# Attention's shift moved out of a matrix product and into spare rows of its operands: a two-block transformer kernel on one Trainium2 core

## What is computed

```python
hd = emb // HEADS                       # 8, HEADS = 16
q = jnp.einsum('bse,oe->bso', x, wq) + bq
qh = q.reshape(HEADS, b, s, hd)
kh = qh
vh = qh
scores = jnp.einsum('hbqd,hbkd->hbqk', qh, kh) / sqrt(emb)
attn = jax.nn.softmax(scores, axis=-1)
out = jnp.einsum('hbqk,hbkd->hbqd', attn, vh)
...
x = x + 0.5 * ffn(ln(x))       # experts, "m0" in the kernel
x = x + attention(ln(x))       # this attention
x = x + 0.5 * ffn(ln(x))       # experts again, "m1"
```

## Time and profile before

| | us |
|---|---|
| median of three runs | 2499.76 |
| the profiled execution, its own time | 2515.66 |
| its span, first to last instruction | 2513.9 |
| outside the span | 1.8 |
| mean granted TensorE clock | 0.909 of full speed |
| TensorE busy | 2036.8 (81%) |
| VectorE busy | 1426.1 (57%) |
| ScalarE busy | 1236.0 (49%) |

### The profile page before, as it was taken

How to read it: one execution, slowest core, us unless ns; L and a number is a source line. 1 busy time by engine, 2 the same in 40 slices (tenths; PEclk the granted TensorE clock), 3 DMA queues, 4 the chain that set the end, 5 groups by cost and what they waited for, 6 DMA issues and landing times.

```text
span 2513.9 us, 38918 instructions
## 1 busy us (share of the span) xinstructions
PE 2036.8 (81%) x13610; PEld 1594.7 (63%) x13610; DVE 1426.1 (57%) x4130; ACT 1236.0 (49%) x2670; POOL 648.7 (26%) x663
## 2 busy tenths in 40 slices
PE   2766773587878888998899889989998999788884
PEld 1555552476557556875787578757875886665764
DVE  5877536453556675566556565666566356356522
ACT  3766413444446455555555564555455446335431
POOL 3111003333131133124223322332233124013052
PEclk9777885699889899999899999999999999899997
DMA  7100000112211211312132213221322312312121
GB/s 237 43 1 1 1 1 0 31 45 64 56 47 44 65 52 57 85 55 55 52 91 57 65 39 89 62 65 32 92 67 60 88 52 68 89 29 61 41 62 47
DMA packets 228948, 141.29 MB, mean 56 GB/s; under 512 B 116489, under 2 KB 206732, under 8 KB 228754
## 3 DMA queue, kind: packets, MB, share of 16 engines
q1 hardware_dynamic: 174320, 85.60, 13.4%
q0 software_dynamic: 16960, 34.74, 4.6%
q10 hardware_dynamic: 37474, 18.46, 2.6%
HBM read 82.48 MB, written 57.16 MB: 56 GB/s over the span
## 4 chain that ended last, share of the span: by engine, by line
PE 53%; DVE 24%; ACT 12%; issue 6%; DMA 2%; POOL 2%; SPq 1%; ACTq 0%; POOLq 0%; DVEq 0%
PE PS L908 17%; PE PS L876 9%; DVE AR L1085 3%; PE PS L1207 3%; PE PS L1170 3%; PE PS L1188 3%; PE PS L1433 2%; PE PS L1193 2%; ACT AR L1141 2%; DVE small L332 2%; ACT AR L837 2%; ACT AR L362 2%; DVE AR L795 2%; DVE xnT L1269 1%; PE PS L911 1%
## 5 line engine op out<-in xcount | busy, mean ns | idle before, releaser
L908 PE MATMUL PS<-AR,W 128*128 128x256 f32 x2560 | 653.0, 404 | 20.9 <-DVE AR L795 15.0
L795 DVE TENSOR_TENSOR AR<-AR,PS 128x512 f32<-128x512 f32 (+1 forms) x384 | 228.6, 597 | 653.9 <-ACT AR L837 525.8
L908 PEld LDWEIGHTS PS<-AR,W 128*128 128x128 f32 x2560 | 499.8, 204 | 92.1 <-issue 17.0
L837 ACT ACTIVATE AR<-PS 128x512 f32<-128x512 f32 (+1 forms) x384 | 201.1, 525 | 556.5 <-PE PS L908 439.1
L1085 DVE TENSOR_REDUCE AR<-PS 128x2 f32<-128x512 f32 x512 | 337.2, 688 | 160.0 <-PE PS L1170 155.6
L1141 ACT ACTIVATE AR<-PS 128x512 f32<-128x512 f32 x512 | 303.6, 600 | 236.3 <-PE PS L1193 231.9
L876 PE MATMUL PS<-AR,WO 128*128 128x256 f32 (+1 forms) x1536 | 357.7, 383 | 0.0
L876 PEld LDWEIGHTS PS<-AR,WO 128*128 128x128 f32 (+1 forms) x1536 | 295.5, 193 | 42.8
L1170 PE MATMUL PS<-AR 128*128 128x256 bf16 x1024 | 204.8, 287 | 40.4 <-DVE AR L1085 25.9
L743 POOL DMA_INDIRECT AR<-YE,gidx1c x128 | 128.8, 1007 | 379.8 <-issue 231.4
L743 POOL DMA_INDIRECT AR<-YE,gidx x128 | 128.3, 1002 | 350.9 <-ACT AR L1141 310.8
(11 more groups left out here) (359 smaller groups left out, 2771.5 us busy)
## 6 DMA issues: line engine op xcount, KB each, us to landing
AR<-XE SPq DMA_DIRECT2D x128, 128.0 KB, 2.1
YE<-AR ACTq DMA_DIRECT2D x128, 128.0 KB
AR<-QD SPq DMA_DIRECT2D x384, 32.0 KB
QD<-AR SPq DMA_DIRECT2D x8, 768.0 KB, 5.2
AR<-KD SPq DMA_DIRECT2D x64, 96.0 KB
W<-in_L_ffn_w_kernel_dram SPq DMA_DIRECT2D x2, 2560.0 KB, 13.5
OD<-AR SPq DMA_DIRECT2D x128, 36.0 KB
X<-in_L_attn_dense_dram SPq DMA_DIRECT2D x8, 512.0 KB, 4.5
```

What stands on the lines that cost most here:

```text
L795: ins = dve.tensor_tensor(hf[:, cols], gl[i % 2][:, cols], H[:, 2 * (i % 2) + 1, cols], ALU.mult)
L837: ins = act.activation(gl[i % 2][:, cols], H[:, 2 * (i % 2), cols], ACT.Gelu_apprx_tanh)
L908: mm = pe.matmul(H[:, b0, b * CAP:(b + 1) * CAP], w0[:, e, hb * P:(hb + 1) * P], xeT[e % 2], start=True, stop=True)
```

## The change

The shift goes into the operands. Rows 64 to 87 of the queries' image, unused so far, take the negated maxima: three parts for each of the 8 blocks. The keys' image holds a mask there that is 1 in the three rows of a key's own block and 0 in the others (`own`, written once for each of the 4 images by ScalarE, `own_act`). `shifted(i)` is then two matmuls, and the two with `pick` go. In detail:

- `scores` needs these rows to be zero in the queries, so each load of a piece has one more DMA, which copies 24 zero rows of the keys' image to them. The six DMAs of the queries become three, with a repeated source.
- `split` writes its parts in another layout; the transpose is two instead of one, and ScalarE's copy (`turned`) is 32x256 instead of 128x128.
- New on VectorE: `place(c)`, a copy of 32 partitions x 2048 bf16 that repeats the 256 negated maxima of each row for all 8 blocks. The first slot of a piece waits for it.
- The scores run up to 16 blocks ahead, and not 14.
- `split` of pieces 1 to 7 stands in slots 3, 8, 16, 24, 32, 40, 48 (before: 3, 11, 19, 27, 35, 43, 51), the transposes and `turned` two slots later, `values` in slots 7, 13, 21, 29, 37, 45, 53 (before: 2, 10, 18, ... 50), and `place` in slots 0, 8, 13, 21, 29, 37, 45, 53 for pieces 0 to 7.

```diff
         def scored(i):
-            return min(NS, i + PB + 6, PB + 2 * (i + 1))
+            return min(NS, i + 2 * PB, PB + 2 * (i + 1))
...
+        SPLIT = [slot_of(PB * (c + 2) - 1) for c in range(NPC - 1)]
+        TURN = [i + 2 for i in SPLIT]
+        VALUES = [TURN[0] + 2] + [i + 3 for i in TURN[1:]]
+        PLACE = [i + 5 for i in SPLIT]
...
-            for lo, hi, a in ((0, 8, 0), (8, 16, 0), (16, 24, 0), (24, 32, 8), (32, 40, 8), (40, 48, 16)):
-                sp.dma_start(QA[c % DEPTH][lo:hi, :], qr[a:a + hi - lo, :]).then_inc(S["a_kq%d" % (c % DEPTH)], 16)
+            for lo, times, part in ((0, 3, 0), (3 * AD, 2, 1), (5 * AD, 1, 2)):
+                rows = qr[part * AD:(part + 1) * AD].rearrange("(o d) t -> o d t", o=1)
+                sp.dma_start(QA[c % DEPTH][lo:lo + times * AD, :], rows.broadcast_to([times, AD, 2 * QUAD])
+                             ).then_inc(S["a_kq%d" % (c % DEPTH)], 16)
+            sp.dma_start(QA[c % DEPTH][SHIFT:SHIFT + 3 * PB, :],
+                         KA[c % DEPTH][ZEROS:ZEROS + 3 * PB].rearrange("p a t -> p (a t)")
+                         ).then_inc(S["a_kq%d" % (c % DEPTH)], 16)
...
+            def place(c):
+                dve.wait_ge(S["a_mp"], NPC * n + c + 1)
+                dve.tensor_copy(QA[c % DEPTH][SHIFTS, :].rearrange("p (g b t) -> p g b t", g=AH, b=PB),
+                                MP[c % 2][SHIFTS, :].rearrange("p (g o t) -> p g o t", g=AH, o=1).broadcast_to(
+                                    [32, AH, PB, AB])).then_inc(S["a_md"], 1)
...
+        def own_act(act, k):
+            view = KA[k][SHIFTS].rearrange("p g (x j) -> p g x j", j=4)
+            act.copy(view, own[SHIFTS, :].rearrange("p (g o j) -> p g o j", g=2, o=1).broadcast_to(
+                [32, 2, QUAD // 4, 4])).then_inc(S["a_kone"], 1)
...
-                act.wait_ge(S["a_mxT"], NPC * n + c + 1)
-                act.copy(MP[c % 2], turned_maxima(c)).then_inc(S["a_mp"], 1)
+                k = NPC * n + c
+                act.wait_ge(S["a_mxT"], k + 1)
+                if k >= 2:
+                    act.wait_ge(S["a_md"], k - 1)
+                act.copy(MP[c % 2][SHIFTS], turned_maxima(c)[SHIFTS]).then_inc(S["a_mp"], 1)
...
-                pe.transpose(turned_maxima(c), MS[c % 2].rearrange("p a b -> p (a b)"),
-                             identb[:, :]).then_inc(S["a_mxT"], 1)
+                for q in range(2):
+                    mm = pe.transpose(turned_maxima(c)[:, q * P:(q + 1) * P], MS[c % 2][:, q, :], identb[:, :])
+                mm.then_inc(S["a_mxT"], 1)
...
+                if b == 0:
+                    pe.wait_ge(S["a_md"], NPC * n + c + 1)
                 for h in range(2):
-                    pe.matmul(o[:, h * 256:(h + 1) * 256], keys(c, P, h, b), queries(c, b), start=(h == 0),
-                              stop=False, skip_group_check=True)
-                if b == 0:
-                    pe.wait_ge(S["a_mp"], NPC * n + c + 1)
-                for q in range(2):
-                    mm = pe.matmul(o.rearrange("p (h q t) -> p q h t", h=2, q=2)[:, q],
-                                   pick[:, q * PB + b:q * PB + b + 1].broadcast_to([P, P]),
-                                   MP[c % 2].rearrange("p (o t) -> p o t", o=1).broadcast_to([P, 2, P]),
-                                   start=False, stop=True, skip_group_check=True)
+                    mm = pe.matmul(o[:, h * 256:(h + 1) * 256], keys(c, P, h, b), queries(c, b), start=True, stop=True)
                 mm.then_inc(S["a_slot"], 1)
...
+                    b.put(*((slot, lambda k=k: own_act(act, k)) for k, slot in enumerate((7, 8, 12, 13))))
```

More of the change, by code:

```diff
@@ L57 @@
 DEPTH = 4
-MROWS = 3 * 2 * PB
+SHIFT = P // 2
+SHIFTS = slice(SHIFT, SHIFT + 32)
+ZEROS = SHIFT + 32
 A_SCALE = float(D) ** -0.5
@@ L121, in build @@
         identb = sb("identb", [P, P], BF16)
-        pick = sb("pick", [P, 2 * PB], BF16)
         join = sb("join", [P, AD], BF16)
+        own = sb("own", [P, PB], BF16)
         tri = sb("tri", [P, P], BF16)
@@ L210, in build @@
         mrest = ar.take((2 * PB,))
-        MS = [ar.take((P // (2 * PB), 2 * PB), BF16) for _ in range(2)]
-        MP = [ar.take((P,), BF16) for _ in range(2)]
+        MS = [ar.take((2, P), BF16) for _ in range(2)]
+        MP = [ar.take((2 * P,), BF16) for _ in range(2)]
         qTf = tmp[:, :, :].rearrange("p a b -> p (a b)")
@@ L1106, in attend_dve @@
                     continue
+                if i == 0:
+                    place(0)
                 for j in range(done, scored(i)):
@@ L1109, in attend_dve @@
                 done = scored(i)
-                if c + 1 < NPC:
-                    if li == 2:
-                        values(c + 1)
-                    if li == 3:
-                        split(c + 1)
+                if i in SPLIT:
+                    split(SPLIT.index(i) + 1)
+                if i in VALUES:
+                    values(VALUES.index(i) + 1)
+                if i in PLACE:
+                    place(PLACE.index(i) + 1)
+        def own_act(act, k):
+            view = KA[k][SHIFTS].rearrange("p g (x j) -> p g x j", j=4)
+            act.copy(view, own[SHIFTS, :].rearrange("p (g o j) -> p g o j", g=2, o=1).broadcast_to(
+                [32, 2, QUAD // 4, 4])).then_inc(S["a_kone"], 1)
         def attend_act(act, n, beside, stored=None):
@@ L1143, in attend_act @@
                     out(i // 16 if i % 16 > 4 else i // 16 - 1, (i // 4 - 1) % 4)
-                if li == 5 and c + 1 < NPC:
-                    turned(c + 1)
+                if i in TURN:
+                    turned(TURN.index(i) + 1)
             if n is not None:
@@ L1150, in values @@
             def values(c):
-                pe.wait_ge(S["a_mp"], NPC * n + max(c, 1))
+                pe.wait_ge(S["a_mp"], NPC * n + c + 1)
                 for b in range(PB):
@@ L1159, in scores @@
             def scores(c, b):
+                if b == 0 and c == 0 and n == 0:
+                    pe.wait_ge(S["a_kone"], DEPTH)
                 if b == 0:
-                    pe.wait_ge(S["a_kq%d" % (c % DEPTH)], 16 * 9 * (NPC // DEPTH * n + c // DEPTH + 1))
+                    pe.wait_ge(S["a_kq%d" % (c % DEPTH)], 16 * 7 * (NPC // DEPTH * n + c // DEPTH + 1))
                 if c >= 1:
@@ L1225, in attend_pe @@
                 shifted(i)
-                if c + 1 < NPC:
-                    if li == 2:
-                        if c == 0:
-                            pe.wait_ge(S["m_ysb"], stored)
-                        values(c + 1)
-                    if li == 5:
-                        maxima(c + 1)
+                if i in TURN:
+                    if i == TURN[0]:
+                        pe.wait_ge(S["m_ysb"], stored)
+                    maxima(TURN.index(i) + 1)
+                if i in VALUES:
+                    values(VALUES.index(i) + 1)
                 if li == 5:
@@ L2495, in _ @@
             ch.step(pool.memset(onesb[:, :], 1.0))
+            ch.step(pool.memset(own[:, :], 1.0))
             ch.step(pool.memset(onesrow[:, :], 1.0))
@@ L2519, in _ @@
                                        pattern=[[1, P]], channel_multiplier=-1))
+            ch.step(pool.affine_select(out=own[:, :], in_=own[:, :], compare_op=ALU.is_ge, fill=0.0, base=-SHIFT,
+                                       pattern=[[-3, PB]], channel_multiplier=1))
             ch.link(pool.affine_select(out=avg, in_=avg, compare_op=ALU.is_ge, fill=0.0, base=0,
                                        pattern=[[-LSEG, NLT]], channel_multiplier=1))
+            ch.step(pool.affine_select(out=own[:, :], in_=own[:, :], compare_op=ALU.is_ge, fill=0.0, base=SHIFT + 2,
+                                       pattern=[[3, PB]], channel_multiplier=-1))
             ch.step(pool.affine_select(out=avg, in_=avg, compare_op=ALU.is_ge, fill=0.0, base=LSEG - 1,
```

19 lines of the change are left out of this document (8 added, 11 removed).

## The result

The changed kernel takes 2577.8 us, the kernel before 2499.6 in the same comparison: ratio 1.030, with a 95% interval from 1.026 to 1.034. It is slower by 3%. The forecast was 2490 us, its range ended at 2530. The profiled execution took 2577.7 us (span 2575.9), 62 us more than the one before.

What follows compares the result with a forecast made beforehand. It took VectorE to bound much of the attention stages. Stages -12.7 us, `own_act` +2 and extra transposes +1 gave -9.7: 2506 us profiled, 2490 as median; own range 2475 to 2508, whole range 2456 to 2530.

Steps and rivals of the forecast that it cites:

- the loads at 0: Loads of each piece: seven DMAs instead of nine, two issues less helping some 0.3 us each; taken as 0, between -1 and +6 us.
- I count 0.7 us for both: `place(1)` and `place(2)` in slots 8 and 13: cost 0.7 us a stage, as the waits that follow take most up.
- the longer lookahead: Scores two blocks further ahead in a stage: two reductions move into VectorE's waiting time, a gain of 1.2 us.
- Gains by the removal: Wide matmuls leaving a typical stage: 1.3 us at 1372-1388, 1.3 at 1388-1422, 0.5 at the end; more at 854 and 2067.
- Rival 1: Attention stages: TensorE really paces them, so the removal is worth its chain share; 2472 us, or 2446 if places hide; chance 0.32.
- `place`, 0.85 us each: VectorE's copy in the stages: 0.70 us plus 0.15 lost around it; `place(4)`, (5), (6) cost 2.6 us a typical stage.
- rival 2: VectorE's `place` runs at less than two elements a cycle: 2518 us at 1.39 us a copy, 2560 at 2.45; chance 0.17.
- Rival 4: Slot 8's wait for reductions, split and place costs what lighter slots save; 2504 us at 2.5 a stage; 0.43 together with the forecast.
- elsewhere a piece has eight slots of time for its load: Loads beyond the program's two recorded TensorE waits: each piece has over 6 us for its load.
- `own_act`: ScalarE's four mask copies in a stage of experts: 1.84 us each, between 0 and 7.4 us in all, taken as 2.
- rival 3: TensorE's clock in the stages falls as its feed gets thinner: +27 us, 2517; sign a clock under 0.9; chance 0.08.
- The signs that it named: Changed kernel's profile, typical stage: VectorE busy about 61 us, its waits for scores down by half from about 10, length 79.

Runs made afterwards that it cites:

- the mended kernel: Changed kernel with loads as before, no zero copy, places ahead of their slots' other VectorE work, the first of a stage in slot 6: ratio 1.014.
- the rest of the tuning: Mended kernel with the earlier lookahead, plus later places one slot earlier, `place(0)` in two pieces and masks written by GpSimd: ratio 1.002 to the kernel before.

## Why the prediction was wrong

Three terms failed: the loads at 0, which cost 28 to 31 us; "I count 0.7 us for both" at slots 8 and 13, where slot 8 alone costs 3.8 us in a typical stage; and the longer lookahead, a gain of 1.2 us a stage that is a loss. Point by point, by its own steps.

- **Gains by the removal**, 1.3 + 1.3 + 0.5 us and more in the stage at 2067. Right in size as a sum (30 us measured alone in the kernel before; the forecast had 3.1 in six stages, 6 and 4 in the others, 29). How it is shared out was less right: in the changed kernel the gain shows at the end of the typical stage, 2.0 us from slot 42 to 63, where four slots take 3.2 us (3.0 forecast, 3.64 before), and is spent in its middle. Rival 1, which wanted the whole chain share of 57 us, falls.
- **"The scores run two blocks further ahead", 1.2 us gained.** Wrong in sign. I moved two reductions into VectorE's later idle time and did not ask what stands behind them in TensorE's order: two more scores ahead of a product, each waiting for a reduction. Alone it costs 0.4 points in the kernel before, 10 us; in the mended kernel, together with the slots that hang on it, 0.9, 23 us.
- **`place`, 0.85 us each, 2.6 a stage.** The copy takes 0.68 to 0.90, 0.74 in the mean: the size was right, rival 2 falls. But the term was priced as VectorE's time, and that is worth 0.2 points (5 us) in the changed kernel, not clear of nothing.
- **"I count 0.7 us for both" places of slots 8 and 13.** This is the step that failed in the stage. Slot 8 costs 3.8 us, and a bit more follows at slots 10 to 14; putting the places first gives 0.9 points back. Rival 4 had the mechanism, at 2.5 us a stage, and I wrote the very row of work (reductions, second split, place) that the trace now shows, then let waits of another engine absorb it. They could not: it is TensorE that waits, and ScalarE behind it.
- **Loads, "I take 0, between -1 and +6".** The largest single miss: 1.1 to 1.2 points, 28 to 31 us, as measured on the later chips. "Two issues less help" was wrong, as the three issues last as long as the six. And "elsewhere a piece has eight slots of time for its load" looked at the pieces inside a stage; the first pieces of a stage have next to none, in seven of eight stages. That the earlier trace rows names only two waits says that the others arrived in time, not by how much. The wait of the first stage grew by 3.1 us, from 6.46 to 9.59, and five that had none got 2.0 to 3.8: by an estimate from these numbers, their margin was about 1 us or none.
- **`own_act`** was right in size (1.89 us each against 1.84); a loss by it can't be told from chance.
- **The clock**, rival 3: it fell as feared, to 0.90 in the typical stage, and to 0.82 and 0.86 in those at 854 and 2067, under the 0.9 that the forecast had set as this rival's sign. But it fell with the gain in the kernel without its shift too, and raising it by more matmuls made the time longer. The clock takes part of the removal's worth, how much was not measured; the 3% are there without its fall.
- **The signs that it named.** VectorE's busy time came out at 62.2 us (61 forecast). Its waits for scores did not halve, 10.2 us before and 10.0 after, and the typical stage is 84 us long and not 79.

The sum of what was mended, in points: loads 1.1, places 0.6 to 0.9, lookahead with its later slots 0.9, and the rest of the tuning 0.4, from 1.031 down to 1.002. Against the 0.989 of the kernel without its shift 1.3 points are left. VectorE's time for the places is 0.6 of them, measured across chips; that the other 0.7 are the longer path from split to placed rows, the second transpose and one more wait in each piece was argued, not tried alone. Also open: the changed kernel with plain loads and the zero copy stayed at 1.028, where the same copy costs the kernel before 0.3 points. Its longer stages go with a lower clock in slots 16 to 24; what lowered it there is not known. Nor is it shown what costs the 1.9 us from slot 16 to 42 of the typical stage, places, order or clock.

## What to carry to other kernels

An operand that is now written by a copy, where it was a separate matmul before, puts the copy's whole queue into the wait: price the work that stands ahead of it on its engine up to the slot that needs it, not its own length. A stage whose first loads arrive without a recorded wait has an unknown margin; before a load is reshaped, bound that margin from the times of issue and of first use, and take any load with a repeated source as later until a run shows otherwise. Of three edits in one change the side ones (loads 28 us or more, lookahead 10) lost more than the main one could win (30), so try them apart.

## What the runs showed of the hardware

DMAs from a source repeated by a zero stride cost SyncE as much as the plain ones that they replace (1.93 us for three against 1.98 for six), and make TensorE wait 15 us more over eight stages; ahead of the first stage the loads of a piece are there 5.1 us after their last issue and not 1.8. The same program takes 3 to 4% longer on some chips: on those, ScalarE's exponentials in the kernel before stand idle 35 us behind "another core or an unknown queue", a releaser that the first chip's profile does not show, and the first and the last stage are 17 to 19 us longer, in the kernel before and in the changed one. Over the 20 profiles the opening alone moved by up to 5 us.
